# Moving one of two scalings per convolution step from VectorE to GpSimd

## The chip, the cores and the metric

The kernel runs on one core of one Trainium2 chip. The metric is the device time of one execution in microseconds, the median of several executions. Inside the core TensorE (PE) multiplies matrices, VectorE (DVE) and ScalarE (ACT) do elementwise work, GpSimd (POOL) does elementwise work too, and SyncE (SP) issues transfers. Each engine works through its own list in order, and the lists are tied together by semaphores alone.

## The reference

Two blocks follow one another: a state-space layer, whose effect is a long causal convolution of each channel, and a block of local and routed attention. The change touches the first one only:

```python
def _layernorm(x, axis=-1, eps=1e-05):
    m = jnp.mean(x, axis=axis, keepdims=True)
    v = jnp.var(x, axis=axis, keepdims=True)
    return (x - m) / jnp.sqrt(v + eps)
...
        powers = jnp.exp(jnp.log(A_bar)[:, :, None] * t)
        K = jnp.einsum('dn,dnl->dl', C * B_bar, powers)
...
        y = jnp.fft.irfft(K_fft[None] * x_fft, n=fft_size, axis=-1)[:, :, :seq_len]
        y = y + D[:, None] * x_t
...
    x = x + _L0_attn_ref(_layernorm(x, axis=-1), L0_attn_log_A, L0_attn_B_param, L0_attn_C, L0_attn_D)
```

x is 8 x 2048 x 512 in float32 (batch, sequence, channels), and the state has 64 entries for each channel.

## The kernel before

The sequence is cut into 16 chunks of 128 positions. `prepare_phase` computes mean and 1/deviation of every row (`mean`, `rstd`, 128 positions x 128 pairs of batch and chunk) and the taps of each channel. `conv_phase` then does the convolution in 32 steps (`it`) of 16 channels; 8 steps make a group of 128 channels, whose inputs lie in `xg[g % 2]`. Within a chunk a channel is multiplied by a 128 x 128 Toeplitz matrix of its taps (`toep`); what comes from earlier chunks goes through the state: the chunk's inputs are summed into a state by `tail` (PE, `sum_states`, L521), a scan over the chunks carries it on (DVE, L411), and PE adds it to the outputs by `cpow` (L542).

Each step has two halves of eight channels, `h` = 0 and 1. The work of step `it`, engine by engine:

- DVE, `step`: the scan for step it+1 (L411); then for each half it waits until PE has made that half's outputs (`y_made`), normalises the same half of step it+2 into `xn` (L395 subtracts the mean, L398 multiplies by `rstd` in place), and adds the outputs of the half to `xg` in two pieces (L403, `add_y`). The buffer `xn[it % 2]` that is refilled is the one PE has just read.
- PE: `sum_states(it+1)` in two halves (L521, each waits for its half of `tail` and of `xn`), `make_y(it)` in two halves (L537 Toeplitz, L542 state), `turn_tails(it+2)` (L508).
- ACT: copies the turned tails out of PSUM (L460), reverses the next Toeplitz matrix `toep_back` that a transfer has brought (L466), and makes the powers two steps ahead (L451).
- POOL: `cpow_back` (L492, waits for the powers of ACT), and `decay_wide` (L496, waits for the scan that read it before).
- SP: one 1 MB transfer of `toep_back` per step (L370). Early in groups 1 to 3 it also stores the group before in four parts (L364), which wait until every L403 of that group is done, and loads the group after into the same buffer (L82).

The semaphore `normed` is counted up by L398 and waited for by PE ahead of each half of L521; `norm_step` is counted up by L395. PE's wait for the second half of `xn` stands behind its first half of L521 and ahead of `make_y`.

Of the kernel before, what the change touches and what calls it, by code (L numbers as in the profile page):

```python
# [12 lines left out]
ALU = mybir.AluOpType  # L13
# [22 lines left out]
SUB = 16  # L36
# [19 lines left out]
def spread(ap, *dims):  # L56

    return bass.AP(tensor=ap.tensor, offset=ap.offset, ap=[list(ap.ap[0])] + [list(d) for d in dims])


def wait(eng, sem, value):

    if not isinstance(value, int) or value > 0:
        eng.wait_ge(sem, value)
# [9 lines left out]
def columns(at, n):  # L74
    return slice(at, at + n) if isinstance(at, int) else bass.ds(at, n)
# [219 lines left out]
def conv_phase(nc, x, keep, kpad, x2, first_group, first_in, new_sem, spent):  # L295
# [8 lines left out]
    with ExitStack() as ctx:  # L304
        sb, ps, _ = open_tensors(nc, ctx)

        def sem(name):
            spent["convolution"].append(new_sem(name))
            return spent["convolution"][-1]

        xg = [first_group, sb("xg1", [P, NCH, BATCH, P])]
        xn = [sb(f"xn{i}", [P, SUB, COLS]) for i in range(2)]
# [17 lines left out]
        tails_turned = sem("tails_turned")  # L330
        tails_made = sem("tails_made")
        powers_made = sem("cpowers_made")
        normed = sem("normed")
        norm_step = sem("norm_step")
        states_summed = sem("states_summed")
        decay_made = sem("decay_made")
# [6 lines left out]
        mean, rstd, cb = keep["mean"], keep["rstd"], keep["cb"]  # L343

        def by_column(a):

            return spread(a[:, :], [0, SUB // 2], [1, COLS])

        with nc.Block() as block:
# [37 lines left out]
            @block.vector  # L387
            def _(v):
                HALF = SUB // 2

                def normalise(g, sub, it, par, h):

                    src = xg[g % 2][:, :, :, columns(sub * SUB + h * HALF, HALF)].rearrange("p c b d -> p b c d")
                    dst = xn[par][:, h * HALF:(h + 1) * HALF, :]
                    nc.vector.tensor_tensor(dst.rearrange("p d (b c) -> p b c d", c=NCH), src, spread(mean[:, :], [NCH, BATCH], [1, NCH], [0, HALF]),  # L395
                                            ALU.subtract).then_inc(norm_step, 1)
                    v.wait_ge(norm_step, it * 2 + h + 1)
                    nc.vector.tensor_tensor(dst, dst, by_column(rstd), ALU.mult).then_inc(normed, 1)  # L398

                def add_y(g, sub, f):  # L400
                    at = xg[g % 2][:, :, :, columns(sub * SUB, SUB)].rearrange(
                        "p c b (q two) -> p two b c q", two=2)[:, f // 2, :, :, f % 2 * 4:f % 2 * 4 + 4]
                    nc.vector.tensor_tensor(at, ps_y[f][:, :, :].rearrange("p q (b c) -> p b c q", c=NCH), at,  # L403
                                            ALU.add).then_inc(y_added, 1)

                def scan(it, par):

                    v.wait_ge(states_summed, it * 2 + 2)
                    v.wait_ge(wide_made, it + 1)
                    wait(v, y_made, (it - 1) * 4)  # L410
                    nc.vector.tensor_tensor_scan(state[par][:, :, :, :].rearrange("p q b c -> p (q b c)"),  # L411
                                                 decay_wide[:, :, :, :].rearrange("p q b c -> p (q b c)"),
                                                 ps_state[:, :, :].rearrange("p q n -> p (q n)"),
                                                 0.0, ALU.mult, ALU.add).then_inc(scanned, 1)

                def step(g, sub, it, par, g_next, sub_next, ahead=True):

                    if ahead:
                        scan(it + 1, 1 - par)
                    for h in range(2):  # L420
                        v.wait_ge(y_made, it * 4 + 2 * h + 2)
                        if g_next is not None:
                            normalise(g_next, sub_next, it + 2, par, h)
                        for f in BANKS[2 * h:2 * h + 2]:
                            add_y(g, sub, f)


                v.wait_ge(x_in[0], 16 * NCH)
                for it in range(2):
                    for h in range(2):  # L430
                        normalise(0, it, it, it, h)
                scan(0, 0)
                for g in range(groups):
                    base = g * SUBS_PER_GROUP
                    with v.Fori(0, SUBS_PER_GROUP // 2 - 1) as s2:
                        for par in range(2):
                            sub = s2 * 2 + par
                            step(g, sub, sub + base, par, g, sub + 2)
                    for par in range(2):
                        sub = SUBS_PER_GROUP - 2 + par  # L440
                        if g + 1 < groups:
                            v.wait_ge(x_in[(g + 1) % 2], 16 * NCH * ((g + 1) // 2 + 1))
                            step(g, sub, base + sub, par, g + 1, par)
                        else:
                            step(g, sub, base + sub, par, None, None, par == 0)
# [35 lines left out]
            @block.gpsimd  # L481
            def _(pool):

                nc.gpsimd.memset(decay_wide[:, :, :, 0:1], 0.0)
                for used in spent["prepare"]:
                    nc.gpsimd.sem_clear(used)

                pool.wait_ge(decay_made, 1)
                for it in range(NSUB):
                    wait(pool, tails_turned, it * 2)  # L490
                    pool.wait_ge(powers_made, it + 1)
                    nc.gpsimd.tensor_tensor(powers_back[:, :, :], powers[it % 3][:, :, 0:CHUNK][:, :, ::-1],  # L492
                                            spread(cb[:, it * SPAIRS:(it + 1) * SPAIRS], [1, SPAIRS], [0, P]),
                                            ALU.mult).then_inc(back_made, 1)
                    wait(pool, scanned, it)
                    nc.gpsimd.tensor_copy(decay_wide[:, :, :, 1:NCH],  # L496
                                          spread(decay[:, it * SPAIRS:(it + 1) * SPAIRS], [1, SPAIRS], [0, BATCH],
                                                 [0, NCH - 1])).then_inc(wide_made, 1)

            @block.tensor  # L500
            def _(pe):
# [11 lines left out]
                def sum_states(it, par):  # L513

                    wait(pe, scanned, it)
                    for q in range(SPAIRS):
                        if q % 4 == 0:
                            pe.wait_ge(tails_made, it * 2 + q // 4 + 1)
                            pe.wait_ge(normed, it * 2 + q // 4 + 1)
                        for two in range(2):  # L520
                            last = nc.tensor.matmul(ps_state[two * STATE:(two + 1) * STATE, q, :],  # L521
                                                    tail[:, q, two * STATE:(two + 1) * STATE], xn[par][:, 2 * q + two, :],
                                                    start=True, stop=True)
                        if q % 4 == 3:
                            last.then_inc(states_summed, 1)
# [20 lines left out]

                turn_tails(0)
                sum_states(0, 0)
                turn_tails(1)
                for it in range(NSUB):  # L550
                    if it + 1 < NSUB:
                        sum_states(it + 1, (it + 1) % 2)
                    make_y(it, it % 2)
                    if it + 2 < NSUB:
                        turn_tails(it + 2)
# [1536 lines left out]
def ssm_then_routed_attention(nc, x, log_A, B_param, C, D, ln_g, ln_b, w_qkv, w_out, null_q, rt_q, rt_kv,  # L2092
# [6 lines left out]
    with ExitStack() as whole:  # L2099
# [3 lines left out]
        with ExitStack() as convolution:  # L2103
            sb, _, new_sem = open_tensors(nc, convolution)
            spent = {"prepare": [], "convolution": []}
            keep |= {n: sb(n, [P, CPAIRS]) for n in ("cb", "log_abar")}
            keep |= {n: sb(n, [P, TILES]) for n in ("mean", "rstd")}
            first_group = sb("xg0", [P, NCH, BATCH, P])
            first_in = convolution.enter_context(nc.semaphore("cx_in0"))
            prepare_phase(nc, x, log_A, B_param, C, D, keep, kpad, first_group, first_in, new_sem, spent)  # L2110
            conv_phase(nc, x, keep, kpad, x2, first_group, first_in, new_sem, spent)
# [49 lines left out]
```

## Time and profile before

| | us |
|---|---|
| median of 3 executions | 5113.38 (5111.05 to 5115.78) |
| profiled execution | 5107.12 |
| span of its trace | 5105.4 |
| of which the convolution's steps, first Toeplitz matmul to last add | 216.8 to 696.9 |

The page of the profile gives PE 89% busy over the whole span, DVE 57%, ACT 46% and POOL 17%. These are averages over stages with different limits; the 32 steps of the convolution fill under a tenth of the span, and in them PE, DVE and the transfers take turns in setting the pace. The timeline lists instructions by start and duration, with the idle time ahead of one and what ended it in brackets; that is the view to read here.

### The profile page before, as it was taken

What the parts mean: (1) busy time and instruction counts of PE and PEld (TensorE: products, weight loads), DVE (VectorE), ACT (ScalarE), POOL (GpSimd) and SP (SyncE); (2) the same over time, 40 slices, a digit from 0 to 9 for tenths busy, and PEclk for the clock granted to TensorE, in tenths of its full rate; (3) what the DMA queues carried; (4) which work ended last, traced back from release to release, by engine and by line L of the source; (5) the groups of instructions that cost most, each with busy time, mean ns of one, the idle gap of its engine ahead of it and who ended that gap; (6) DMA issues with size and microseconds to landing.
All of it is one profiled execution on the core that took longest, in us unless ns stands there. A gap on an engine that the chain in (4) does not pass through costs nothing. (4 is left out here: it accounts for less than half of the span.)

```text
span 5105.4 us, 84431 instructions
## 1 busy us (share of the span) xinstructions
PE 4530.0 (89%) x31042; PEld 3796.7 (74%) x31042; DVE 2919.7 (57%) x5364; ACT 2366.0 (46%) x5678; POOL 869.0 (17%) x678
## 2 busy tenths in 40 slices
PE   6676757999999999999999999643999999999999
PEld 6566656888888888888888888542777777777776
DVE  5676645555555555555555555577546546546545
ACT  4433324555555555555555555422434434434434
POOL 0112211222222222222212221210011111111111
PEclk9987878999999999999999999755999999999999
DMA  6766751000100000000010000100111121121110
GB/s 217 208 169 173 183 153 34 30 30 26 30 30 26 30 30 26 30 30 26 30 30 26 30 30 16 48 0 17 36 46 22 34 47 22 34 47 22 34 38 11
DMA packets 283807, 268.03 MB, mean 52 GB/s; under 512 B 14704, under 2 KB 212592, under 8 KB 283376
## 3 DMA queue, kind: packets, MB, share of 16 engines
q1 hardware_dynamic: 271088, 228.77, 16.0%
q0 software_dynamic: 12288, 33.56, 3.2%
q8 instruction: 265, 4.34, 0.4%
q14 instruction: 166, 1.36, 0.1%
HBM read 169.49 MB, written 76.02 MB: 48 GB/s over the span
## 5 line engine op out<-in xcount | busy, mean ns | idle before, releaser
L1141 POOL TENSOR_TENSOR l_prob<-l_prob,l_inv 128x768 f32<-128x768 f32 x256 | 370.7, 1470 | 1921.8 <-DVE l_inv L1084 1921.8
L931 ACT ACTIVATE l_prob<-l_ps_s,l_neg_max 128x192 f32<-128x192 f32 (+1 forms) x1024 | 411.8, 429 | 357.7 <-DVE l_neg_max L1068 357.3
L1919 ACT ACTIVATE h_prob<-h_ps_s,h_neg_max 128x1024 f32<-128x1024 f32 x256 | 286.0, 1117 | 341.5 <-DVE h_neg_max L2001 310.4
L1998 DVE TENSOR_REDUCE h_neg_max<-h_ps_s 128x1 f32<-128x1024 f32 x256 | 313.4, 1224 | 201.7 <-PE h_ps_s L1785 199.5
L667 PE MATMUL l_ps_b<-w_qkv_hi,l_xt_hi 128*128 128x512 f32 x1024 | 417.7, 408 | 5.6 <-DVE l_xt_lo L988 2.9
L669 PE MATMUL l_ps_b<-w_qkv_hi,l_xt_lo 128*128 128x512 f32 x1024 | 406.4, 397 | 0.0
L668 PE MATMUL l_ps_b<-w_qkv_lo,l_xt_hi 128*128 128x512 f32 x1024 | 406.3, 397 | 0.0
L828 PE MATMUL l_ps_s<-l_k_t,l_q_t 128*128 128x192 f32 (+2 forms) x2432 | 373.1, 308 | 19.4 <-issue 14.4
L828 PEld LDWEIGHTS l_ps_s<-l_k_t,l_q_t 128*128 128x128 f32 x2432 | 349.8, 191 | 28.1 <-issue 28.1
L1094 DVE TENSOR_TENSOR l_q_t<-l_ps_a,w_bias_q 64x512 f32<-64x512 f32 x256 | 176.2, 688 | 264.4 <-PE l_ps_a L818 261.7
L1797 PE MATMUL h_ps_t<-ident,h_prob 128*128 128x128 f32 x2048 | 277.4, 278 | 7.6 <-ACT h_prob L1919 7.6
L1809 PE MATMUL h_ps_o<-h_probs_t,h_val 128*64 128x128 f32 x4096 | 278.4, 279 | 0.0
L1809 PEld LDWEIGHTS h_ps_o<-h_probs_t,h_val 128*64 128x64 f32 x4096 | 218.5, 136 | 80.1 <-issue 53.0
L1797 PEld LDWEIGHTS h_ps_t<-ident,h_prob 128*128 128x128 f32 x2048 | 222.6, 140 | 60.5 <-issue 43.3
L1087 DVE COPY l_pt_side<-l_ps_c 64x512 f32<-64x512 f32 x128 | 88.9, 695 | 291.1 <-PE l_ps_c L834 291.1
L1081 DVE COPY l_pt_main<-l_ps_c 128x512 f32<-128x512 f32 x128 | 88.6, 692 | 270.5 <-PE l_ps_c L834 270.5
L2055 DVE COPY h_probs_t<-h_ps_t 128x512 f32<-128x512 f32 x256 | 176.5, 689 | 107.6 <-PE h_ps_t L1797 104.2
L1068 DVE TENSOR_REDUCE l_neg_max<-l_ps_s 128x4 f32<-128x768 f32 (+1 forms) x256 | 227.1, 926 | 13.0 <-PE l_ps_s L828 13.0
L1784 PE MATMUL h_ps_s<-h_k,h_q_hi 128*128 128x512 f32 x512 | 223.8, 437 | 6.8 <-ACT h_val L1940 6.8
L667 PEld LDWEIGHTS l_ps_b<-w_qkv_hi,l_xt_hi 128*128 128x128 f32 x1024 | 193.5, 189 | 48.0 <-ACT l_q_tok L938 4.6
L669 PEld LDWEIGHTS l_ps_b<-w_qkv_hi,l_xt_lo 128*128 128x128 f32 x1024 | 193.4, 189 | 46.3
L668 PEld LDWEIGHTS l_ps_b<-w_qkv_lo,l_xt_hi 128*128 128x128 f32 x1024 | 193.9, 189 | 40.4
(358 smaller groups left out, 11166.5 us busy)
## 6 DMA issues: line engine op xcount, KB each, us to landing
xin<-in_L_attn_x_dram SPq DMA_DIRECT2D x32, 1024.0 KB, 5.2
xg<-in_L_attn_x_dram SPq DMA_DIRECT2D x64, 512.0 KB, 9.4
toep_back<-taps_padded SPq DMA_DIRECT2D x32, 1024.0 KB, 8.4
x<-xg SPq DMA_DIRECT2D x64, 512.0 KB, 7.6
l_xin<-x SPq DMA_DIRECT2D x128, 256.0 KB, 2.9
out_dram<-l_res SPq DMA_DIRECT2D x128, 256.0 KB, 2.0
h_q_hi<-h_q_hi SPq DMA_DIRECT2D x64, 128.0 KB, 5.5
h_q_lo<-h_q_lo SPq DMA_DIRECT2D x64, 128.0 KB, 6.1
```

Of the source, the lines that this page charges most:

```text
L667: nc.tensor.matmul(out, lh, rh, start=first, stop=False)
L668: nc.tensor.matmul(out, lh, rl, start=False, stop=False)
L669: return nc.tensor.matmul(out, ll, rh, start=False, stop=last)
L828: last = nc.tensor.matmul(ps_s[:, win, pair, col:col + n], q_t[:, j % RING, pair, win, :], k_t[:, pair, key:key + n], start=True, stop=True)
L931: last = nc.scalar.activation(prob[jt % 2][:, pair, AT[win] + lo:AT[win] + hi], ps_s[:, win, pair, lo:hi], ACT.Exp, bias=neg_max[:, jt % 2 ...
L1068: nc.vector.tensor_reduce(neg_max[:, jt % 2, win, :], ps_s[:, win, :, lo:hi], AX_X, ALU.max, negate=True).then_inc(max_made, 1)
L1141: nc.gpsimd.tensor_tensor(mine, mine, spread(inv[:, jt % 2, win, :], [1, PAIRS], [0, MAIN + SIDE]), ALU.mult).then_inc(p_normed, 1)
L1784: nc.tensor.matmul(ps_s[i % 2][:, half, :], q2_hi[:, h, rows], k2[:, h, cols], start=True, stop=False)
L1797: last = nc.tensor.transpose(ps_t[half][:, n, :], prob[i % 2][:, at:at + P], ident[:, :])
L1809: last = nc.tensor.matmul(ps_o[odd * DH:(odd + 1) * DH, k * P:(k + 1) * P], val[:, n, h * DH:(h + 1) * DH], probs_t[(2 * pair + odd) % 4][ ...
L1919: nc.scalar.activation(prob[i % 2][:, :].rearrange("p (a k) -> p a k", a=2), ps_s[i % 2][:, :, :], ACT.Exp, bias=neg_max[:, qt % 2, h:h + ...
L1998: nc.vector.tensor_reduce(at, ps_s[i % 2][:, :, :].rearrange("p a k -> p (a k)"), AX_X, ALU.max, negate=True).then_inc(max_step, 1)
```

## The change

GpSimd multiplies the second half of each step's `xn` by `rstd`; VectorE keeps the two subtractions and the first multiplication. `normed` becomes two semaphores, one for each half, as the halves now come from different engines. GpSimd's new instruction stands at the end of its step, behind `decay_wide`, and waits for the subtraction of that half.

```diff
-        normed = sem("normed")
+        normed = [sem(f"normed{h}") for h in range(2)]
...
-                    v.wait_ge(norm_step, it * 2 + h + 1)
-                    nc.vector.tensor_tensor(dst, dst, by_column(rstd), ALU.mult).then_inc(normed, 1)
+                    if h == 0:
+                        v.wait_ge(norm_step, it * 2 + 1)
+                        nc.vector.tensor_tensor(dst, dst, by_column(rstd), ALU.mult).then_inc(normed[0], 1)
...
+                    half = xn[it % 2][:, SUB // 2:SUB, :]
+                    pool.wait_ge(norm_step, it * 2 + 2)
+                    nc.gpsimd.tensor_tensor(half, half, by_column(rstd), ALU.mult).then_inc(normed[1], 1)
...
-                            pe.wait_ge(normed, it * 2 + q // 4 + 1)
+                            pe.wait_ge(normed[q // 4], it + 1)
```

`by_column(rstd)` reads the same 128 numbers of a partition once for each of the 8 channels, so the innermost run of this operand is 128 different numbers in a row.

VectorE's list in the second half of a step, from the wait for `y_made` to the next scan, before:

```order
L421 REGISTER_ALU
L395 ISA [waits y_made]
L395 TENSOR_TENSOR xn<-xg,mean 128x128x8
L397 REGISTER_ALU
L398 TENSOR_TENSOR xn<-xn,rstd 128x1024 [waits norm_step]
L403 ISA
L403 TENSOR_TENSOR xg<-ps_y,xg 128x8x16x4
```

and after (the lines have moved by one):

```order
L422 REGISTER_ALU
L395 ISA [waits y_made]
L395 TENSOR_TENSOR xn<-xg,mean 128x128x8
L404 ISA
L404 TENSOR_TENSOR xg<-ps_y,xg 128x8x16x4
```

The two adds of the half (L403, now L404) follow the subtraction directly.

GpSimd's list for one step, before:

```order
L492 TENSOR_TENSOR cpow_back<-cpow,cb 128x1024 [waits cpowers_made,tails_turned]
L496 COPY decay_wide<-decay 128x64x15 [waits scanned]
```

and after, with the first instruction of the step behind it:

```order
L493 TENSOR_TENSOR cpow_back<-cpow,cb 128x1024 [waits cpowers_made,tails_turned]
L497 COPY decay_wide<-decay 128x64x15 [waits scanned]
L502 TENSOR_TENSOR xn<-xn,rstd 128x1024 [waits norm_step]
L493 TENSOR_TENSOR cpow_back<-cpow,cb 128x1024 [waits cpowers_made,tails_turned]
```

The scaling of step it stands between `decay_wide` of that step and `cpow_back` of the next.

## Rows read from the trace of the kernel before

**Rows 1.** Windows over the steps that follow one another without a wait for transfers
```profile
core 0: us, PE busy (x) PEld busy (x) DVE busy (x) ACT busy (x) POOL busy (x), PEclk, DMA share, GB/s
216.83:308.44 91.61, 77.99 (x786) 70.71 (x784) 78.05 (x63) 37.40 (x78) 19.95 (x14) 0.93 0.66 173
435.78:448.74 12.96, 10.23 (x115) 9.26 (x113) 12.00 (x9) 7.13 (x18) 4.43 (x2) 1.00 0.38 104
562.66:682.29 119.63, 97.50 (x1011) 88.22 (x1009) 105.92 (x81) 50.46 (x100) 34.21 (x18) 0.95 0.61 150
```

**Rows 2.** Waits, 100 to 850 us: who for whom, total us, times, longest
```profile
POOL cpow_back L492 <- ACT cpow L451: 359.3, 31, 22.0
...
ACT toep L466 <- DMA toep_back<-taps_padded: 108.8, 14, 14.9
...
PE ps_state L521 <- DVE xn L398: 38.5, 20, 2.7
```

**Rows 3.** Timeline of one step, VectorE: start us, us, engine, line [idle before]
```profile
258.54 2.40 DVE L395 TENSOR_TENSOR xn<-xg,mean 128x1024 f32<-128x1024 f32 x1 [0.72 <-PE ps_y L542]
...
263.31 1.98 DVE L395 TENSOR_TENSOR xn<-xg,mean 128x1024 f32<-128x1024 f32 x1
265.33 1.22 DVE L398 TENSOR_TENSOR xn<-xn,rstd 128x1024 f32<-128x1024 f32 x1
266.47 1.28 DVE L403 TENSOR_TENSOR xg<-ps_y,xg 128x512 f32 x2
268.01 2.29 DVE L411 TENSOR_TENSOR_SCAN state<-decay_wide,ps_state 128x1024 f32<-128x1024 f32 x1 [0.25 <-PE ps_state L521]
```

**Rows 4.** Timeline of the same step, TensorE
```profile
255.25 2.05 PE L537 MATMUL ps_y<-xn,toep 128*128 128x128 f32 x16
257.23 1.16 PE L542 MATMUL ps_y<-state,cpow 64*128 64x120 f32 x16
...
266.70 1.09 PE L521 MATMUL ps_state<-xn,tail 128*64 128x128 f32 x16 [2.24 <-DVE xn L398]
267.72 3.67 PE L537 MATMUL ps_y<-xn,toep 128*128 128x128 f32 x16
```

**Rows 5.** Groups of two-input GpSimd instructions: count | busy us, mean ns | idle before
```profile
L1141 POOL TENSOR_TENSOR l_prob<-l_prob,l_inv 128x768 f32<-128x768 f32 x256 | 370.7, 1470 | 1921.8 <-DVE l_inv L1084 1921.8
L1145 POOL TENSOR_TENSOR l_xin<-l_xin,w_row 128x512 f32<-128x512 f32 x128 | 165.2, 1290 | 114.7 <-ACT l_xn L906 114.7
...
L1198 POOL TENSOR_TENSOR w_k_lo<-hw_raw_parts,w_k_hi 128x2048 fp32r<-128x2048 f32 x1 | 4.5, 4494 | 0.0
```

**Rows 6.** Timeline, GpSimd's results waited for, and waiting for VectorE
```profile
242.80 2.29 DVE L411 TENSOR_TENSOR_SCAN state<-decay_wide,ps_state 128x1024 f32<-128x1024 f32 x1 [1.12 <-PE ps_state L521]
245.15 0.98 POOL L496 COPY decay_wide<-decay 128x960 f32<-128x960 f32 x1 [0.71 <-DVE state L411]
...
340.84 1.90 POOL L492 TENSOR_TENSOR cpow_back<-cpow,cb 128x1024 f32<-128x1024 f32 x1 [16.18 <-ACT cpow L451]
...
342.79 3.64 PE L508 MATMUL ps_tail<-ident,cpow_back 128*128 128x128 f32 x16 [3.39 <-POOL cpow_back L492]
```

**Rows 7.** Groups of the two VectorE instructions, whole convolution: count | busy us, mean ns
```profile
L395 DVE TENSOR_TENSOR xn<-xg,mean 128x1024 f32<-128x1024 f32 x64 | 136.9, 2140 | 43.7 <-PE ps_y L542 31.1 <-PEq L139 12.6
...
L398 DVE TENSOR_TENSOR xn<-xn,rstd 128x1024 f32<-128x1024 f32 x64 | 86.9, 1358 | 2.2
```

**Rows 8.** Timeline, a place where GpSimd and VectorE meet
```profile
634.31 1.23 DVE L398 TENSOR_TENSOR xn<-xn,rstd 128x1024 f32<-128x1024 f32 x1
634.40 2.90 POOL L492 TENSOR_TENSOR cpow_back<-cpow,cb 128x1024 f32<-128x1024 f32 x1 [7.66 <-ACT cpow L451]
...
635.45 1.29 DVE L403 TENSOR_TENSOR xg<-ps_y,xg 128x512 f32 x2
...
636.65 2.46 DVE L395 TENSOR_TENSOR xn<-xg,mean 128x1024 f32<-128x1024 f32 x1
```

**Rows 9.** Timeline, last adds of group 0 and the first store
```profile
319.77 1.28 DVE L403 TENSOR_TENSOR xg<-ps_y,xg 128x512 f32<-128x512 f32 x2
...
321.08 5.37 SPq L364 DMA_DIRECT2D x<-xg  x4
```

## The prediction

> **What bounds the kernel now.** The averages of the page don't decide here: the change lies in the 32 steps of the convolution, so I read first how long their stretches are, then who waits for whom in them, then one step in the timeline, instruction by instruction.
>
> The steps are of two kinds. In some, the Toeplitz matrix arrives late: ACT's L466 waited 108.8 us for `toep_back` in 14 steps [rows 2], because stores and loads of `xg` stand in the same transfers. They are paced by the transfers: between the stretches of [rows 1] 7 steps take 127.3 us (308.44 to 435.78) and 6 take 113.9 (448.74 to 562.66), 18 to 19 us each; something that is later on DVE or POOL there costs nothing as long as it fits into the wait. Three stretches lie outside of this: 216.83 to 308.44 (7 steps), 435.78 to 448.74 (1 step) and 562.66 to 682.29 (9 steps), each from the first Toeplitz matmul of one step to that of another. Their 17 steps take 91.61 + 12.96 + 119.63 = 224.2 us [rows 1], 13.2 us each. Some of the last nine have short transfer waits too, but the next paragraph's chain ends as late.
>
> What closes the circle in such a step is seen where PE waits: 20 times, 38.5 us in all, PE stood before the second half of L521 until DVE's L398 had ended [rows 2]. Follow one step from 255.25. PE makes the first half of the outputs until about 258.3 [rows 4]. DVE then starts L395 at 258.54 and goes through subtraction, scaling, two adds, subtraction, scaling without a gap; the last scaling begins at 265.33 and takes 1.22, so it ends at 266.55 [rows 3]. PE has been idle for 2.24 us, starts the second half of L521 at 266.70, and begins the next `make_y` at 267.72 [rows 4]. So the circle is PE's half of L521, PE's first half of outputs, and DVE's whole list up to and with **the second scaling**, 12.47 us in this step. The two adds behind it (266.47) and the scan (268.01) are off it: ahead of its first L395 DVE has the scan behind it and waits 0.72 us for PE's outputs [rows 3].
>
> **The change, part by part.** The instruction that moves is the last one of the circle. DVE loses 1.23 us per step, but the work stays on the circle, on a slower engine.
>
> *How long POOL takes.* The trace has no GpSimd instruction of just this form, so I bound it. Two families show. Where the second input is one number repeated along the innermost run, 1024 elements take 1.90 us (L492 [rows 6]) and 768 take 1.470 (L1141 [rows 5]). Where both inputs run through different numbers, 512 take 1.290 and 2048 take 4.494 [rows 5], which is (4.494 - 1.290) / 1536 = 2.09 ns for each further element, so 1.290 + 512 x 2.09 ns = 2.36 us for 1024. `rstd` is read as runs of 128 different numbers, so I take **2.36**; 1.90 is the lower bound, and 2.58 (twice the 1.290 of 512) the upper.
>
> The Trainium skill (GPSIMD Engine Reference, 3.1 Elementwise) gives 4497 ns for a two-input instruction of 2048 float32 elements and says that such work belongs on VectorE, which is about twice as fast. The row of L1198 agrees with its figure (4494 [rows 5]). Halved, it would give 2.25 us and a term smaller by 1.9 us below; nothing here rests on it.
>
> *The handovers.* After a DVE instruction POOL starts 0.06 us later (scan 242.80 + 2.29 = 245.09, L496 at 245.15 [rows 6]); PE starts 0.05 after POOL (340.84 + 1.90 = 342.74, L508 at 342.79 [rows 6]). Before, the scaling began 0.04 after the subtraction and PE 0.15 after the scaling [rows 3, 4]; from the subtraction's end at 265.29 to PE's start at 266.70 it was 1.41. Now it is 0.06 + 2.36 + 0.05 = 2.47. That is **+1.06 us** on the circle of a step, with 1.90 it would be +0.60, with 2.58 +1.28. Times 17 steps: **+18.0 us** (10.2 to 21.8).
>
> *Less collision.* DVE's L395 and L398 are stretched where POOL works at the same time. Undisturbed they take 1.98 and 1.22 [rows 3]; their means over 64 are 2.140 and 1.358 [rows 7], so the stretching is 64 x 0.16 + 64 x 0.138 = 19.1 us over 32 steps, and 17/32 of it, 10.1 us, lies in the steps that count. In the new steps DVE has one such instruction less, and the circle is longer while ACT's powers are not, so L492 starts earlier against the scan and less of it and of L496 falls on L395. Where a transfer makes the powers late the collision stays, but a longer circle meets that less often. I take a bit more than half: **-6 us** (0 to -9).
>
> *The stores start earlier.* The first store of a group waits for its last L403: adds from 319.77 to 321.05, store at 321.08 [rows 9]. These adds now follow the subtraction directly, 1.14 us earlier against their own step (265.33 to 266.47 [rows 3]). The transfers set the pace from there on, so the stretch behind it starts and ends 1.14 earlier, three times: **-3.4 us**. Within these stretches POOL's scaling costs nothing: ACT's wait for `toep_back`, 7.8 us on average (108.8 / 14 [rows 2]), covers 1.06.
>
> *Nobody else waits longer on POOL.* Behind the new wait POOL has `cpow_back` of the next step. It is released by ACT's powers, and PE needs it only after `make_y`. POOL stood waiting for those powers 31 times, 359.3 us in all [rows 2], 11.6 us each; the scaling's 2.36 fall into that, and without this cover PE's `make_y` of two halves (3.1 us each [rows 4]) would still hide it. `decay_wide` stands ahead of the scaling and waits for a scan that is over by then. At the very start DVE saves two scalings and POOL has them to do among its first two `cpow_back`: about 0, give or take 1.5.
>
> *TensorE's clock.* The mean granted clock is 0.93 and 0.95 in the long stretches [rows 1]: PE falls to the lower level (1.2 of 2.4 GHz) now and then after its idle time, as at 267.72, where 16 matmuls took 3.67 instead of 2.05 us after 2.24 us idle [rows 4]. That costs 1.6 us, on the circle. By the means, PE was at the lower level for 2 x 0.07 x 91.6 + 2 x 0.05 x 119.6 = 24.8 us on the 17 steps, some seven groups like this one. The idle time grows from about 2.2 to 3.3 us, so more steps may be hit; but part of the slower time then falls into the idle time itself. I count the cost as unchanged, 0, with 3 drops fewer (-5) to 5 more (+8) as bounds.
>
> **Sum:** 18.0 - 6 - 3.4 = +8.6, say **+9 us** on the profiled execution's 5107.12, that is 5116. The median is 5113.38, 6 above that execution, so I forecast 5122. A measurement of this kernel can tell about 0.2% from no change, 10 us; +9 is +0.18%, just inside.
>
> **Rivals.**
> 1. *More drops of the clock.* For it: a longer idle time ahead of each second half of L521, in every step alike. Against it: a step that is slowed leaves PE idle for less time, and the stretch of one step ran at 1.00 [rows 1]. Five more drops, 5 x 1.6 = +8, give 5130. It decides if 12 or so of the 17 steps are hit.
> 2. *The adds block GpSimd.* POOL's scaling runs beside two adds of DVE, 1.29 us together. If they held it up as L398 does, each step would be longer by about 1.2, +20 us: 5142. For it: at 634.40 L492 took 2.90 instead of 1.90, as L398 was running until 635.54. Against it, in the same row: from 635.54 its 1.9 us ran beside the adds (635.45, 1.29, not stretched), to 637.30; only then L395, with both inputs in SBUF, became longer (2.46) [rows 8]. The Trainium skill (SBUF — State Buffer, Who interferes with whom) says that a VectorE instruction shares GpSimd's read port only if both its inputs are in SBUF; L403 has one in PSUM. The trace agrees: 2.90 is 1.90 and 1.0 of L398.
> 3. *Not slower, the other side.* GpSimd takes 1.90 after all (it depends on how it reads `rstd`), and the relief is whole: 10.2 - 9 - 3.4 = -2, so 5111, on the far side of no change. It decides at 1.90 to 2.0 us for the new instruction. Against it: both groups with two running inputs are slower per element than both with a repeated one [rows 5, 6].
> 4. *Faster.* DVE with 1.23 us less would have to be the bound by its sum. It isn't: it waits for PE at both ends of its list [rows 3]. To gain 10 us the new instruction would have to take about 1.3 us.
>
> **How the numbers follow.** The forecast's case (2.2 to 2.4 us, drops about as before) has 0.55, and a third of it lies over +10 us, as +9 is near the edge. Rival 1 has 0.22, most of it over +10; rival 2 has 0.05; rival 3 has 0.15, within 0.2%; rival 4 has 0.03. Slower: 0.18 + 0.18 + 0.05 = 0.41. Same: 0.37 + 0.04 + 0.15 = 0.56. Faster: 0.03. The range goes from the middle between rival 3 and the forecast to rival 1, 5114 to 5131; the 0.2 left out are the rest of rival 3, rival 2, and rival 4.
>
> **What would show it.** Right: a GpSimd group `xn<-xn,rstd` x32 of mean 2.3 to 2.4 us, L398's successor x32; PE's wait ahead of L521 now put down to POOL `xn`, some 55 us in all in place of 38.5; a step like the one followed here at about 13.3 us in place of 12.47; the first stores 1.1 us earlier against the `make_y` of their step; L395's mean under 2.14. Wrong: a mean of 1.90 (term 1 is then 10), or of over 3 (the adds block it); the count of slowed Toeplitz groups far from seven; the steps that wait for transfers longer than before, which I count as fixed.

## The result, and the profile after

| | us |
|---|---|
| before, median of 4 executions | 5112.22 (5110.05 to 5115.78) |
| after, median of 4 executions | 5143.32 (5142.17 to 5144.37) |
| ratio, 95% interval | 1.0060 (1.0043 to 1.0078) |
| profiled execution of after, span of its trace | 5144.37, 5142.3 |

The changed kernel is slower by 31 us. The forecast was 9 us, and its range ended at 5131. (Here and below the ratio compares runs of the same round, so it isn't exactly the quotient of the medians.)

First, where in the span do the 31 us lie? The first matmul of the next stage comes behind the convolution, after a wait for its weights that is 45.2 us long in both kernels. Its line in before, then in after; the columns are the duration in ns (least, median, most) and the first and the last start in us:

```profile
L607 PE MATMUL lw_ps_bias<-lw_b,lw_raw x96: 342/352/352, 740.8 to 761.1; 128*128 128x1 f32 x96
```
```profile
L611 PE MATMUL lw_ps_bias<-lw_b,lw_raw x96: 343/352/353, 773.8 to 794.1; 128*128 128x1 f32 x96
```

The next stage starts at 773.8 in place of 740.8, 33.0 us later. From there to the end it is 4364.6 us before and 4368.5 after. So nearly all of it is in the convolution; the start of this stage will be the measure of every experiment too, as it is free of what the later stages do.

Windows over the same steps as in [rows 1], kernel after; `PEclk` is the granted clock:

```profile
core 0: us, PE busy (x) PEld busy (x) DVE busy (x) ACT busy (x) POOL busy (x), PEclk, DMA share, GB/s
216.16:320.67 104.51, 82.71 (x786) 74.74 (x784) 68.91 (x56) 39.18 (x84) 39.05 (x22) 0.87 0.61 157
449.65:465.02 15.37, 11.12 (x115) 9.98 (x113) 11.07 (x8) 7.48 (x19) 8.65 (x4) 0.88 0.48 136
578.54:715.33 136.79, 108.07 (x1010) 97.72 (x1008) 90.42 (x72) 50.09 (x100) 52.53 (x27) 0.86 0.54 132
```

The 17 steps take 256.7 us in place of 224.2 [rows 1], that is +32.5. The 13 steps between them, in which the transfers set the pace, take 129.0 and 113.5 in place of 127.3 and 113.9. The column to look at is PEclk: 0.87, 0.88 and 0.86, where it was 0.93, 1.00 and 0.95. As in the prediction, the means give the time at the lower level: 2 x (0.13 x 104.5 + 0.12 x 15.4 + 0.14 x 136.8) = 69 us, where it was 25.

The groups of the convolution, kernel after (count | busy us, mean ns | idle before, and what ended it):

```profile
L541 PE MATMUL ps_y<-xn,toep 128*128 128x128 f32 x1024 | 154.9, 313 | 0.0
...
L395 DVE TENSOR_TENSOR xn<-xg,mean 128x1024 f32<-128x1024 f32 x64 | 133.5, 2088 | 57.9 <-PE ps_y L546 45.6 <-PEq L139 12.3
...
L525 PE MATMUL ps_state<-xn,tail 128*64 128x128 f32 x1024 | 89.2, 332 | 72.9 <-POOL xn L502 72.5 <-issue 0.2 <-DVE xn L399 0.2
```

and the two PE groups of before:

```profile
L537 PE MATMUL ps_y<-xn,toep 128*128 128x128 f32 x1024 | 141.5, 295 | 0.0
...
L521 PE MATMUL ps_state<-xn,tail 128*64 128x128 f32 x1024 | 76.6, 302 | 41.8 <-DVE xn L398 38.5 <-DVE state L411 3.2
```

The same matmuls, untouched by the change, take 13.4 and 12.6 us longer, **26.0 us** together. Of 64 Toeplitz groups (two in each step, 2.05 us each at full clock) 19 take more than 2.2 us; before there were 8. I call these slowed. Not all of the 26.0 us lengthens the kernel, as part of it falls into steps that wait for transfers anyway (busy us of the two groups, before and after, from windows of each line alone):

| | length | Toeplitz | state sums | slowed groups |
|---|---|---|---|---|
| the 17 steps | 224.2, 256.7 | 77.4, 83.7 | 39.4, 49.2 | 6, 11 |
| the 13 steps between | 241.3, 242.5 | 55.0, 62.1 | 30.9, 34.6 | 1, 7 |

So **16.1 us** of slower matmuls stand in the steps that became longer by 32.5.

One step in PE's timeline, kernel after (start us, us, what, in brackets the idle time ahead and what ended it):

```profile
304.10 1.82 PE L525 MATMUL ps_state<-xn,tail 128*64 128x128 f32 x16 [2.96 <-POOL xn L502]
305.85 2.93 PE L541 MATMUL ps_y<-xn,toep 128*128 128x128 f32 x16
308.70 1.16 PE L546 MATMUL ps_y<-state,cpow 64*128 64x120 f32 x16
309.79 2.05 PE L541 MATMUL ps_y<-xn,toep 128*128 128x128 f32 x16
```

Compare it with [rows 4]. After 2.24 us of idle time the second half of L521 ran at 1.09, and the Toeplitz group behind it was hit. Now PE is idle for 2.96 us, and the second half of L525 is hit as well (1.82), which is 0.73 more, with 0.88 for the Toeplitz group: 1.61 in all, as much as the 1.62 of [rows 4]. But the next step is hit for longer: its half of L525 takes 1.97 (below) and its Toeplitz group 3.78, together 2.6 us more than at full clock. Both lie on the circle of the step. The steps of group 0 are 13.8 to 15.8 us long; before they were 12.5 to 13.6.

The other steps of the circle, from the end of such a step to the start of the next circle, kernel after, all engines:

```profile
314.22 1.96 DVE L395 TENSOR_TENSOR xn<-xg,mean 128x1024 f32<-128x1024 f32 x1
316.03 1.29 DVE L404 TENSOR_TENSOR xg<-ps_y,xg 128x512 f32<-128x512 f32 x2
316.27 2.35 POOL L502 TENSOR_TENSOR xn<-xn,rstd 128x1024 f32<-128x1024 f32 x1 [6.92 <-DVE xn L395]
318.77 1.97 PE L525 MATMUL ps_state<-xn,tail 128*64 128x128 f32 x16 [2.84 <-POOL xn L502]
```

The subtraction ends at 316.18, the scaling runs from 316.27 to 318.62, and PE starts at 318.77: 0.09 + 2.35 + 0.15 = 2.59, where it was 1.41 from [rows 3] to [rows 4].

### The profile page after: what moved, and what is told of

It is laid out like the page before. It is cut to its first block and busy times, and to the rows that moved or that the text cites. A ratio compares the mean times of both kernels' runs of the same rounds, so it can differ in the third digit from the quotient of the medians.

```text
span 5142.3 us, 84420 instructions
## 1 busy us (share of the span) xinstructions
PE 4558.5 (89%) x31042; PEld 3820.0 (74%) x31042; DVE 2869.6 (56%) x5332; ACT 2362.1 (46%) x5678; POOL 944.0 (18%) x710
```

## Experiments

Two theories were set against each other. *The clock*: the longer wait for the scaling makes PE idle for longer in every step, and then more of its matmuls run at the lower of its two levels, 1.2 in place of 2.4 GHz. *Interference*: it is GpSimd's work beside VectorE (and two semaphores in place of one) that costs. Where the quoted expectations use letters, A is the clock and B interference. `next stage` is the start of the matmul shown above, from the profiled execution of each kernel; `slowed` is the number of Toeplitz groups of over 2.2 us among 64.

| kernel | median us | ratio to before, 95% | next stage | slowed |
|---|---|---|---|---|
| before | 5112.22 | | 740.8 | 8 |
| after | 5143.32 | 1.0060 (1.0043 to 1.0078) | 773.8 | 19 |
| e4_split_sem | 5112.97 | 0.9997 (0.9988 to 1.0007) | 741.0 | 7 |
| e3_before_extra_dve | 5147.71 | 1.0058 (1.0041 to 1.0075) | 781.1 | 20 |
| e1_before_fill12 | 5104.45 | 0.9982 (0.9973 to 0.9992) | 737.1 | 0 |
| e2_after_fill20 | 5127.97 | 1.0027 (1.0017 to 1.0037) | 758.2 | 0 |
| e5_before_fill6 | 5106.52 | 0.9982 (0.9972 to 0.9992) | 732.0 | 0 |
| e6_after_fill10 | 5110.98 | 0.9996 (0.9986 to 1.0005) | 738.5 | 0 |
| e9_after_fill4 | 5126.34 | 1.0023 (1.0013 to 1.0032) | 752.3 | 7 |
| e7_no_scaling | 5087.91 | 0.9944 (0.9922 to 0.9966) | 726.2 | 6 |
| e8_pool_first_half | 5121.25 | 1.0013 (1.0004 to 1.0023) | 748.7 | 10 |
| e10_before_adds_late | 5100.78 | 0.9969 (0.9958 to 0.9981) | 730.1 | 6 |
| e11_after_adds_late | 5116.89 | 1.0004 (0.9992 to 1.0015) | 743.0 | 7 |
| e12_adds_late_fill3 | 5093.29 | 0.9960 (0.9948 to 0.9971) | 722.9 | 0 |

### The semaphores alone

e4 has the two semaphores of the change, but VectorE does both scalings:

```diff
-                    if h == 0:
-                        v.wait_ge(norm_step, it * 2 + 1)
-                        nc.vector.tensor_tensor(dst, dst, by_column(rstd), ALU.mult).then_inc(normed[0], 1)
+                    v.wait_ge(norm_step, it * 2 + h + 1)
+                    nc.vector.tensor_tensor(dst, dst, by_column(rstd), ALU.mult).then_inc(normed[h], 1)
```

> Only the semaphore normed is split in two; both scalings stay on VectorE. Both theories: 5112 within 4 us. If it is slower by more, the two semaphores and not the engine are part of the cost.

Measured: the time of before, and the next stage at 741.0. So the semaphores cost nothing that can be measured here.

### The same delay without GpSimd

e3 is the kernel before, with one more VectorE instruction of 1.23 us between the second scaling and PE's wait (the larger of `xn` and itself, which changes nothing). GpSimd does no more than before:

```diff
-                    nc.vector.tensor_tensor(dst, dst, by_column(rstd), ALU.mult).then_inc(normed, 1)
+                    if h == 0:
+                        nc.vector.tensor_tensor(dst, dst, by_column(rstd), ALU.mult).then_inc(normed, 1)
+                    else:
+                        nc.vector.tensor_tensor(dst, dst, by_column(rstd), ALU.mult).then_inc(again, 1)
+                        v.wait_ge(again, it + 1)
+                        nc.vector.tensor_tensor(dst, dst, dst, ALU.max).then_inc(normed, 1)
```

> The kernel before, with one more VectorE instruction of 128x1024 (maximum of the second half of xn with itself, which changes nothing, 1.23 us) between the second scaling and PE's wait. The circle is longer by 1.25 us as in the change (1.17), without GpSimd. Theory A: as slow as the change or a little slower, 5140 to 5150, with PE's clock down in nearly every step. Theory B: only the circle's 17 x 1.25 = 21 us, 5133, and the clock as before.

Measured: 5147.71, as slow as the change. Window over the first seven steps, PE's wait (us in total, times, longest) and its timeline, kernel e3:

```profile
218.26:324.11 105.85, 84.50 (x787) 76.43 (x785) 85.56 (x70) 37.33 (x77) 19.55 (x15) 0.85 0.59 148
```
```profile
PE ps_state L527 <- DVE xn L404: 74.5, 23, 4.5
```
```profile
306.43 1.98 PE L527 MATMUL ps_state<-xn,tail 128*64 128x128 f32 x16 [3.14 <-DVE xn L404]
308.33 3.78 PE L543 MATMUL ps_y<-xn,toep 128*128 128x128 f32 x16
```

The wait of 74.5 us is that of the change (72.5), the clock is 0.85 (0.87), and the two groups behind the idle time are slowed alike. GpSimd isn't needed for the loss; interference as the cause falls.

### The clock held up by matmuls that nobody needs

If the idle time is what lowers the clock, matmuls put into it must give the time back, although PE then has more to do. The filler multiplies the identity by itself into a part of `ps_tail` that ACT has already copied out, behind PE's wait for `tail` and ahead of its wait for the second half of `xn`:

```diff
                             pe.wait_ge(tails_made, it * 2 + q // 4 + 1)
+                            if q == 4:
+                                for _ in range(10):
+                                    nc.tensor.matmul(ps_tail[:, 7, :], keep["ident"][:, :], keep["ident"][:, :],
+                                                     start=True, stop=True)
                             pe.wait_ge(normed[q // 4], it + 1)
```

The first two tries took too many.

> The kernel before, with 12 matmuls of the identity with itself (128 columns each, into a part of ps_tail that ACT has read) ahead of PE's wait for the second half of xn. They fill some 1.5 us of the 2.2 us in which PE stands idle there. Theory A (the clock: PE's idle time ahead of that wait brings its clock down, and the slower Toeplitz matmuls behind it lie on the circle): the some seven slowed groups vanish from the 17 steps outside the transfer waits, 7 x 1.6 = 11 us less, 5101 us, mean granted clock there 0.99 or more. Theory B (the clock is not what costs; the change's extra 13 us come from GpSimd and VectorE in each other's way, or from the new waits): no gain, 5112 or a few us more.

> The changed kernel, with 20 such matmuls in the same place (2.6 us of the 2.9 us idle there). Theory A: the longer circle stays (17 steps x 1.17 us = 20 us, less some 5 for fewer collisions), the clock's share goes: 5143 falls to 5115 to 5122, and the difference to the kernel before with such matmuls is 15 to 20 us. Theory B: it stays at 5140 or above.

Measured: e1 5104.45, e2 5127.97. No group is slowed in e1, but its clean steps are all 13.04 us long, and those of e2 14.83: a filler takes 0.24 us, twelve take 2.9 and twenty 4.7, more than the idle time, so PE itself closes the circle; both came out above the times that I had given (5101, and 5115 to 5122). Even so e2, with 20 useless matmuls in each step, is 15 us faster than the changed kernel. The next pair was sized to leave some half a microsecond of idle time.

> The kernel before with 6 filling matmuls instead of 12. The first try showed that one takes 0.236 us there, so 12 took 2.8 us and PE itself closed the circle at 13.04 us a step; 6 take 1.4 us of the 2.2 idle. Theory A: the clock stays up and PE is not the bound, so a step outside the transfer waits takes 12.0 to 12.5 us, 17 x 0.8 = 13 us less than before: 5098. If the clock were not what costs: 5112, or the 5104 of 12 fillers at best.

> The changed kernel with 10 filling matmuls (2.4 us of the 2.9 idle). Theory A: clock up, a step at 13.1 to 13.5 us, so 5114 to 5120, and 15 to 20 us above the kernel before with 6 fillers: that difference is the longer circle alone (17 x 1.17 us = 20, less collisions). Theory B (GpSimd and VectorE in each other's way): at 5128 as with 20 fillers, or above.

Measured: e5 5106.52 and e6 5110.98. Windows over the first seven steps, first e5, then e6:

```profile
216.28:302.12 85.84, 82.38 (x871) 74.53 (x869) 79.16 (x63) 37.74 (x80) 19.86 (x14) 1.00 0.71 186
```
```profile
214.56:308.25 93.69, 88.64 (x926) 80.79 (x924) 69.77 (x56) 38.53 (x82) 36.79 (x22) 1.00 0.67 173
```

One step of e6; L525 is the filler here (its ten matmuls have two records each), L529 the state sum:

```profile
304.18 2.50 PE L525 MATMUL ps_tail<-ident 128*128 128x128 f32 x20
304.81 2.37 POOL L502 TENSOR_TENSOR xn<-xn,rstd 128x1024 f32<-128x1024 f32 x1 [6.26 <-DVE xn L395]
...
307.23 1.09 PE L529 MATMUL ps_state<-xn,tail 128*64 128x128 f32 x16 [0.55 <-POOL xn L502]
```

The changed kernel with ten useless matmuls in each step is 32 us faster than without (5110.98 and 5143.32), and its next stage starts 35.3 us earlier. The scaling still takes 2.37; the idle time is 0.55, the state sum 1.09, the clock 1.00. This also splits the loss. With the clock held up on both sides, the change costs 738.5 - 732.0 = **6.5 us** in the convolution (4.5 by the medians). Without it, it cost 33.0. So **26.5 us** go with the drops of the clock. That this is close to the 26.0 by which the two PE groups grew is no proof, as 16.1 of those lie in the steps that count. The split depends on the transfers: with the clock held up they close some steps that the circle closed before, and hide part of its length. The last nine steps take 119.9 us in e5 and 119.6 in the kernel before, so there nothing was won by the fillers. Counted within the two kernels themselves, the clock's part is 16.1 of 32.5 us, and the longer circle is the rest. By either count the clock costs 16 to 26 us.

Both runs missed what I expected: e5 is 8 us above my 5098, e6 3 below its range, and they lie 4.5 us apart in place of 15 to 20. e5 alone, 6 us under the kernel before, wouldn't decide between the theories; e6 does. In the first seven steps the difference is as expected (85.84 and 93.69, 1.12 for each step); the rest is hidden as just said.

e9 takes four fillers, so that some 2 us of the idle time stay (49.8 us in 24 waits):

> The changed kernel with 4 filling matmuls: 0.9 of the 2.9 us of PE's idle time is filled, 2.0 is left, about as long as in the kernel before. Theory A (it is the length of the idle time that brings the clock down): between no filling (5143) and 10 (5111), with some steps slowed and some not, as before the change: 5118 to 5130, and the next stage's first matmul (L607 of before) at 745 to 762 us, where it is at 773.8 without and at 738.5 with 10. If a step of over 13 us lets the clock down whatever the idle time: 5138 or more.

Measured: 5126.34, next stage at 752.3, clock over the first seven steps:

```profile
216.89:312.27 95.38, 81.69 (x842) 73.50 (x840) 69.02 (x56) 38.07 (x80) 37.55 (x22) 0.97 0.65 172
```

With 0, 4 and 10 fillers the kernel after takes 5143, 5126 and 5111; 19, 7 and 0 Toeplitz groups are slowed. The traces of all 14 kernels say the same, if PE's last idle time ahead of each step's first Toeplitz group is sorted by length (those that end with a state sum, L521 or its successor):

| idle time | times | slowed group behind it |
|---|---|---|
| under 1.4 us | 92 | 0 |
| 1.4 to 1.85 | 41 | 3 |
| 1.85 to 2.7 | 70 | 35 |
| over 2.7 | 63 | 52 |

The kernel before has 19 such idle times over 1.4 us, of which 8 were followed by a slowed group; the kernel after has 22, all over 2.7, and 19 were.

### Without the second scaling

In e7 the second half of `xn` isn't scaled at all, so its outputs are another function; PE waits for the subtraction alone. It shows what that scaling is worth.

```diff
-                                            ALU.subtract).then_inc(norm_step, 1)
+                                            ALU.subtract).then_inc(norm_step if h == 0 else normed[1], 1)
...
-                    pool.wait_ge(norm_step, it * 2 + 2)
-                    nc.gpsimd.tensor_tensor(half, half, by_column(rstd), ALU.mult).then_inc(normed[1], 1)
```

> The scaling of the second half is left out altogether (its inputs stay unscaled), on both engines; PE waits for the subtraction. The circle is shorter by 1.25 us a step. Theory A: 17 x 1.25 = 21 us from the circle, unless the scan (which ends 0.7 us ahead of the first half of the outputs) takes over, so 12 to 21, and 5 to 10 from the clock, as PE's idle time falls to about 1 us: 5085 to 5095. If the circle were not what sets the pace: 5105 or more.

Measured: 5087.91, clean steps of 11.4 to 12.3 us. More than some 25 us wasn't to be gained at this place, not even by a scaling that costs nothing.

### The other half on GpSimd

In e8 GpSimd scales the first half of a step, which has some time left before PE needs it, and VectorE the second:

```diff
-                    if h == 0:
+                    if h == 1:
...
-                    half = xn[it % 2][:, SUB // 2:SUB, :]
+                    half = xn[it % 2][:, 0:SUB // 2, :]
```

> GpSimd scales the first half of each step's channels and VectorE the second: the same instruction, the same 2.36 us, at another place of the circle. VectorE's two adds (1.2 us) and then its next subtraction stand behind it; the subtraction has both inputs in SBUF and is held up until GpSimd is done. Theory A: subtraction to subtraction is 2.4 us in place of the 2.3 of scaling and adds, so the circle stays within 0.2 us and the time within 4 us of before, 5110 to 5116, with a subtraction of the second half some 1.2 us longer. If GpSimd's share in itself cost the change's time: 5135 or more.

Measured: 5121.25, so 22 us faster than the change, though GpSimd does the same work, but at least 5 slower than I expected. Two readings of its timeline, first a clean step, then the end of a stretch that waits for transfers:

```profile
251.09 1.29 DVE L404 TENSOR_TENSOR xg<-ps_y,xg 128x512 f32 x2
...
251.33 2.37 POOL L502 TENSOR_TENSOR xn<-xn,rstd 128x1024 f32<-128x1024 f32 x1 [3.19 <-DVE xn L395]
...
252.36 3.19 DVE L395 TENSOR_TENSOR xn<-xg,mean 128x1024 f32<-128x1024 f32 x1
```
```profile
427.91 2.14 POOL L493 TENSOR_TENSOR cpow_back<-cpow,cb 128x1024 f32<-128x1024 f32 x1 [7.64 <-ACT cpow L452]
430.00 2.58 POOL L497 COPY decay_wide<-decay 128x960 f32<-128x960 f32 x1
432.55 3.33 POOL L502 TENSOR_TENSOR xn<-xn,rstd 128x1024 f32<-128x1024 f32 x1
```
```profile
436.03 3.30 PE L525 MATMUL ps_state<-xn,tail 128*64 128x128 f32 x32 [3.86 <-POOL xn L502]
```

In the clean step the adds (251.09) aren't stretched beside L502, but the next subtraction is: 3.19 in place of 1.96. That eats the 1.23 us which VectorE saves; steps without a slowed group and without a wait for transfers stay at 12.0 to 12.8. The Trainium skill (SBUF — State Buffer, Who interferes with whom) says that a two-input VectorE instruction contends with GpSimd's reads if both inputs are in SBUF and not if only one is; both rows agree with it. The second reading is the part I had missed: where the powers come late, GpSimd's scaling stands behind `cpow_back` and `decay_wide`, and PE waits 3.86 us for it. Steps of this sort are 16.1 to 17.8 us long in four places, with such waits of 3.0 to 3.9 us.

### Shortening the circle instead

Of the circle's list on VectorE [rows 3] the first two adds have no hurry. e10 is the kernel before with the adds of both halves behind the second scaling, e11 the changed kernel with the same edit:

```diff
-                        for f in BANKS[2 * h:2 * h + 2]:
+                        if g_next is None:
+                            for f in BANKS[2 * h:2 * h + 2]:
+                                add_y(g, sub, f)
+                    if g_next is not None:
+                        for f in BANKS:
                             add_y(g, sub, f)
```

> The kernel before with VectorE's first two adds of a step moved behind its second scaling (subtract, scale, subtract, scale, four adds). No engine gets other work; 1.2 us leave the circle. Theory A: the circle goes from 12.0 to about 11 us a step (VectorE's own list, 2.3 scan + 6.3 + 2.4, is then the bound) and PE's idle time falls to 1 us, so the clock stays up: 12 to 20 us less from the circle, up to 10 from the clock, 5085 to 5098. If neither is what sets the pace: 5108 or more.

> The changed kernel with the same order: VectorE's four adds (2.4 us) now run beside GpSimd's scaling (2.36). The circle is that of the change less 1.2 us: 12.0 us a step as in the kernel before. PE's idle time is then about 1.8 to 2 us. Theory A: 5100 to 5115, some 25 to 35 us less than the change, and 12 to 20 us more than the kernel before in this order. If GpSimd's work were what costs: 5130 or more.

Measured: 5100.78 and 5116.89, both some 2 or 3 us slower than the ranges I gave. PE's timeline of e10:

```profile
250.86 1.09 PE L525 MATMUL ps_state<-xn,tail 128*64 128x128 f32 x16 [1.15 <-DVE xn L398]
251.89 2.05 PE L541 MATMUL ps_y<-xn,toep 128*128 128x128 f32 x16
```

The idle time is 1.15 us here, and 0.4 to 1.3 in twelve steps in all, none of which has a slowed group; the six that are slowed come after some 2 us or more, in other steps. Clean steps take 11.3 to 11.6, as the adds' 1.28 are off the circle. Moving the scaling to GpSimd costs 16 us here (5116.89 - 5100.78), half of the 31 that it costs with the adds where they were; by the next stage it is 12.9, where it was 33.0. PE's idle time in e11 is 1.6 to 2.4 in most steps, and 7 groups are slowed in place of 19. So the same move has two prices. The clock has a part in that, as it brings one more slowed group here and eleven there; the transfers, which pace some of e10's last nine steps (18.8 us for one), have another, and no run here parts the two.

e12 adds three fillers to e10:

> The kernel before with the late adds of e10 and, besides, 3 filling matmuls (0.7 us) ahead of PE's wait for the second half of xn. In e10 PE was idle there for 1.2 us in some steps and 2.0 in others, and three Toeplitz groups (2.57, 3.49, 3.27 us) and more of the steps behind were slowed. Theory A: the slowed steps outside the transfer waits vanish, 5 to 8 us less than e10 in the convolution, its following stage starting at 722 to 726 us instead of 730.1, and 5092 to 5098. If what is left is the transfers' pace alone: as e10, 5100, stage start 729 or later.

Measured: 5093.29, the fastest kernel here with all of the computation: 20 us under the kernel before in the same rounds (5113.92), 50 under the changed one. No group is slowed; where the circle closes a step, the idle time is mostly about 0.3 us and the step 11.4.

## Why the prediction was wrong

The forecast was +9 us, within 0.2%, with 0.41 for slower; measured were +31, 12 us over the end of the range. What failed is the term for TensorE's clock, put at 0: it was 16 to 26 us. By the prediction's own steps:

- **What bounds the kernel** was right. The scaling was the last link of the circle, and e3 (one more instruction at this place, +36 us) and e7 (one less, -24) show it from both sides.
- **How long POOL takes**: 2.36 forecast from [rows 5], measured over 32 instructions (least, median, most in ns):

```profile
L502 POOL TENSOR_TENSOR xn<-xn,rstd x32: 2345/2356/3323, 203.8 to 711.1; 128x1024 f32<-128x1024 f32 x32
```

- **The handovers** were nearly right: +1.18 per step in place of +1.06. POOL starts 0.09 after the subtraction (I took 0.06), and PE 0.15 after POOL (I took 0.05 from [rows 6]; it was the 0.15 of DVE to PE that carries over).
- **The 17 steps** are right only as long as the clock falls. 17 x 1.18 = 20.1, less 4.1 for collisions (below), and with the 16.1 of slower matmuls is 32.1, close to the 32.5 measured; in part by luck, as in the kernel before three of the last nine hardly waited for the scaling (0.6 us twice, and not at all). With the clock held up they are too many: e6 is 7.85 us slower than e5 over the first seven steps, 1.12 each, as worked out, but over the last nine only 2.2 (122.1 and 119.9), since in e5 some of them wait for the transfers (one takes 18.3 us). I had written that "the next paragraph's chain ends as late"; there it doesn't.
- **Less collision**: L395's mean fell from 2140 [rows 7] to 2088 ns, which is 3.3 us, and the second scaling's share of the stretching of L398 went away with it (32 x 0.14 = 4.4). Together 7.7 over 32 steps, so 4.1 in 17 if they are spread evenly; I took 6.
- **The stores earlier**: they were, but against the step only by nothing. The first store starts at 333.24, 12.57 us behind the Toeplitz matmul that opens its step (320.67); before it was 321.08 - 308.44 = 12.64 [rows 1, 9]. The 1.1 us of the moved adds had gone into the slowed group of 3.78 us that opens that step. The stretches behind took 129.0 and 113.5, 1.3 us more and not 3.4 less. With the clock held up the term is there: the first store of e6 starts 10.86 us behind the opening of its step and that of e5 12.25, and e6 takes 125.4 and 111.5 for the stretches, e5 128.2 and 112.0.
- **Nobody else waits longer on POOL** held for the change (PE's waits for `cpow_back` are 91.0 us, 112.4 before). It fails for e8, where a scaling that PE needs early stands behind the powers.
- **TensorE's clock** is the step that failed: "I count the cost as unchanged, 0", with -5 to +8 as bounds. It was **+16 to +26**. I had the row for it in hand: [rows 4] show a drop after 2.24 us of idle time, and the same text has the idle time grow to 3.3. The bound of five more drops was right for the 17 steps (6 slowed groups became 11, where I had put seven); the value of 0 and the price of 1.6 us each were not. All eight drops of the kernel before cost 1.5 to 1.6 us, the half of L521 and the Toeplitz group taken together. Of the 19 after the change nine still do, and ten cost 2.1 to 2.6: in these the half of L525 takes 1.97 in place of 1.09, and the Toeplitz group behind it still 3.3 to 3.8. My argument against it was that a slowed step leaves PE idle for less time. That is so, but not by enough: behind a slowed step the idle time is 1.7 to 1.8 us before and 2.7 to 3.0 after, and 13 of 16 such steps of the kernel after were slowed again, as the rows at 304.10 and 318.77 show.
- **Rival 1** had the mechanism, and its five more drops in the 17 steps were the right number (11 were hit; it had asked for 12 or so). At 1.6 us each they reached only 5130. **Rival 2** (the adds block GpSimd) is false: 1.29 for the adds and 2.35 for the scaling side by side. **Rival 3** needed a scaling of 1.90.

With the clock held up the change costs 6.5 us in the convolution, near the 8.6 of my sum, which had no cost for the clock. That is in part luck: the handovers were too small by 2 us and the relief too large by 2, and what the transfers hide in the last nine steps made up for both. Of what was to show it, "some 55 us" of waiting for POOL's `xn` came out as 72.5 us in 25 waits. What stays open is why a certain step is hit with some 2 us of idle time, and its neighbour isn't: in the kernel before, the next groups ran at full clock after 2.38 us and were slowed after 1.96 (timeline of before):

```profile
228.42 1.09 PE L521 MATMUL ps_state<-xn,tail 128*64 128x128 f32 x16 [2.38 <-DVE xn L398]
229.44 2.05 PE L537 MATMUL ps_y<-xn,toep 128*128 128x128 f32 x16
...
240.61 1.98 PE L521 MATMUL ps_state<-xn,tail 128*64 128x128 f32 x16 [1.96 <-DVE xn L398]
242.51 2.74 PE L537 MATMUL ps_y<-xn,toep 128*128 128x128 f32 x16
```

No experiment here tells them apart.

## What to carry to other kernels

When a change lengthens the wait ahead of PE in a loop, don't price the wait alone: look in the rows after which idle times PE's next groups are slowed already, and where the new one is longer than these, price nearly every step as slowed (19 of 22 idle times here), and for longer than the drops that the rows show. A filler of useless matmuls in the idle time, sized to leave some tenths of a microsecond, is a cheap test (it gave 32 us back here) and a remedy, but shortening the wait by taking work without hurry out of the chain gave more on the kernel before (12 us against 6), and the two add up (20). Work moved to a slower engine helps only if it is off the circle, and its place in that engine's list has to be followed in the steps where that engine is late, too.

## What was not expected of the hardware

- The price of idle time isn't proportional to it. Idle times of about 2 us that became about 3 took the clock of the first seven steps from 0.93 to 0.87 and slowed eleven more groups; from e10 to e11, where idle times of 0.4 to 2.1 became mostly 1.6 to 2.4, one more was slowed. The Trainium skill (TensorE: Matmul & The Clock Gate, Loop structure matters more than you think) says that the loop nest decides whether the matmuls keep their clock. Here the nest is the same in every kernel, and still 0 to 20 groups are slowed: what stands within the body decides as well, down to the order of VectorE's adds (8 groups before, 6 in e10) and three fillers (0 in e12).
- A PE that does more is done earlier: PE's busy time over the first seven steps is 88.6 us in e6 and 82.7 in the kernel after, and the steps take 93.7 and 104.5.
- GpSimd takes 2.36 us for 1024 elements where both inputs run through different numbers, and 1.90 where the second is a repeated number [rows 6]; the same shape in the trace isn't the same price.
- Medians of the kernel before lay between 5110.9 and 5113.9, and its single executions from 5102 to 5127. In the profiled execution of e5 the convolution is 8.8 us shorter than in that of before, but what follows is 14.5 longer, with no edit there. So the start of the next stage was the better measure of these edits, though it has one execution for each kernel.
